# Expert rows weighted on their way out of PSUM and added onto the branch rows by accumulating scatters; the gate dot product as a 257th column

## What is computed

```
abel = gelu(xn @ abel_w + abel_b)
topw, topi = top_k(xn @ moe_gate_w + moe_gate_b, 2);  topw = softmax(topw)
eo[e] = gelu(xn @ ew1[e] + eb1[e]) @ ew2[e] + eb2[e]          # 8 experts, 256 -> 512 -> 256
moe  = sum of eo over a token's two experts, by their weights, times three matrix exponentials
gate = sigmoid(concat(abel, moe) @ gc_w + gc_b)
out  = layernorm-like result of (x + abel * (1 - gate) + moe * gate)
```

## Time and profile before

| | us |
|---|---|
| median of 3 runs (lowest, highest) | 943.55 (942.94, 944.96) |
| the profiled execution | 945.53 |
| its span, first to last instruction | 943.8 |
| PE busy in the span | 720.9 (76%) |
| DVE busy | 585.4 (62%) |
| ACT busy | 386.0 (41%) |
| POOL busy | 252.0 (27%) |
| mean granted clock of TensorE | 0.876 of full speed |

### The profile page before, as it was taken

How to read it: one execution, slowest core, us unless ns; L and a number is a source line. 1 busy time by engine, 2 the same in 40 slices (tenths; PEclk the granted TensorE clock), 3 DMA queues, 4 the chain that set the end, 5 groups by cost and what they waited for, 6 DMA issues and landing times. The chain is left out here.

```text
span 943.8 us, 15614 instructions
## 1 busy us (share of the span) xinstructions
PE 720.9 (76%) x4757; PEld 521.2 (55%) x4758; DVE 585.4 (62%) x1547; ACT 386.0 (41%) x637; POOL 252.0 (27%) x289
## 2 busy tenths in 40 slices
PE   4896759887988889897957308969999999947430
PEld 3785335545464636363635107858888888834220
DVE  5824476859686868879755154644545454507996
ACT  3221537563737365656532102334444444411223
POOL 1000120202516070615152130003333333322332
PEclk9999779999999989999979557989999999975555
DMA  5600223432717263453531128734434443219752
GB/s 156 215 0 0 45 80 54 113 66 85 163 36 188 47 173 76 143 105 108 119 91 68 46 98 276 259 57 104 102 84 102 90 109 80 70 32 346 234 190 89
DMA packets 144447, 106.13 MB, mean 112 GB/s; under 512 B 76416, under 2 KB 134667, under 8 KB 144396
## 3 DMA queue, kind: packets, MB, share of 16 engines
q1 hardware_dynamic: 127980, 75.85, 28.7%
q0 software_dynamic: 16416, 29.64, 13.4%
HBM read 55.05 MB, written 33.62 MB: 94 GB/s over the span
## 5 line engine op out<-in xcount | busy, mean ns | idle before, releaser
L1456 POOL DMA_INDIRECT scratch_ys<-ye,place x78 | 76.9, 986 | 197.8 <-ACT ye L1485 185.1
L52 PE MATMUL up<-xe_s,w_s 128*128 128x256 bf16 x936 | 110.9, 276 | 7.0 <-DMA xe_s<-scratch_zs 7.0
L52 PE MATMUL down<-w_s,h_s_e 128*128 x936 | 108.8, 273 | 0.3 <-DVE h_s_e L1521 0.3
L52 PEld LDWEIGHTS up<-xe_s,w_s 128*128 x936 | 92.7, 99 | 19.4 <-issue 7.5
L52 PEld LDWEIGHTS down<-w_s,h_s_e 128*128 128x128 bf16 x936 | 90.8, 98 | 12.4 <-issue 1.0
L52 PE MATMUL bank<-xn_s,mlp_w 128*128 128x512 bf16 x384 | 89.4, 392 | 10.3 <-DVE xn_s L702 10.3
L1518 DVE CAST h_s_e<-hf_e 128x512 bf16<-128x512 f32 x78 | 35.0, 448 | 98.7 <-ACT hf_e L1475 98.6
L391 POOL DMA_INDIRECT scratch_zs<-rows,pos x64 | 77.3, 1207 | 61.4 <-DVE pos L860 42.6
L52 PE MATMUL bank<-mlp_w,shared 128*128 128x256 bf16 x768 | 86.4, 273 | 2.2 <-DVE shared L758 2.2
L1475 ACT ACTIVATE hf_e<-up,eb 128x256 f32<-128x256 f32 x156 | 65.5, 471 | 48.0 <-PE up L52 47.4
L52 PEld LDWEIGHTS bank<-mlp_w,shared 128*128 128x128 bf16 x768 | 74.9, 98 | 12.7 <-DVE shared L758 2.7
(11 more groups left out here) (239 smaller groups left out, 1278.5 us busy)
## 6 DMA issues: line engine op xcount, KB each, us to landing
w_f<-in_ew SPq DMA_DIRECT2D x16, 512.0 KB, 5.5
got<-scratch_ys SPq DMA_DIRECT2D x16, 512.0 KB, 6.1
x_in<-in_x SPq DMA_DIRECT2D x8, 512.0 KB
x_ob<-in_out_b_row SPq DMA_DIRECT2D x8, 512.0 KB, 3.8
x_res<-in_mlp_b_row SPq DMA_DIRECT2D x8, 512.0 KB, 4.9
x_ob<-in_x POOLq DMA_DIRECT2D x8, 512.0 KB, 8.8
x_res<-in_x POOLq DMA_DIRECT2D x8, 512.0 KB, 10.9
x_res<-x POOLq DMA_DIRECT2D x8, 512.0 KB, 5.2
```

The lines of the kernel that those rows point to most:

```text
L52: last = nc.tensor.matmul(dst, lhs(a, k), rhs(b, k), start=start and n == 0, stop=stop and n == total - 1)
L1456: nc.gpsimd.indirect_dma_start(out=ys_dram[:, :], out_offset=bass.IndirectOffsetOnAxis(ap=place[:, k, s:s + 1], axis=0), in_=ye[:, k % 2, ...
```

## The change

The weights of a token's two experts are now made batch by batch in the first stage (`weigh`) and ride with the row into `zs`, negated, as two more tags. In the expert stage DVE reads from the tags which of the two weights a row needs, and ACT multiplies by it while it copies the row out of PSUM. POOL's scatters add (`compute_op=ALU.add`) onto `ys`, which has one row for each token and starts as the stored `abel` row, so that it ends as `abel - moe`. Since two tiles can add to the same row, POOL waits for the scatters of the tile before. The folded `eb2` is added inside the expert's PSUM group by a matmul over two rows (`ones2`, `eb2_s`). Every row has a 257th column: the weight stage appends `turnmat` times `gc_w` as a column, so that PE computes the gate's dot product with the row; `abel`'s part is stored as its row's 257th number. The rows of `eb2` are moved to one partition and split at the end of the weight stage. `abx` is loaded into SBUF at the end of the expert stage. The last stage has no PE work, no `weighted` and no difference on POOL. `dots` and `store_branch` of the first stage now follow each other, since the stored row holds the dot product.

```diff
+HOME, FIRST, SECOND_W, MORE_W = 2 * D, 2 * D + 2, 2 * D + 4, 2 * D + 6
+DG = D + 1
 ROW = 2 * D + 16
...
                         .then_inc(z4T_in, 16)
             def store_branch(j):
-                sp.wait_ge(gelu_r, TT * j + TT)
-                sp.dma_start(ab_dram[j].rearrange("(t p) d -> p t d", p=P), abel[j % 2])\
...
                 pool.wait_ge(rows_tail, j + 1)
...
                 nc.scalar.activation(az[:, :], az[:, :], ACT.Ln, bias=1.0).then_inc(lz_r, 1)
+                if i >= LAG:
...
+                    nc.vector.scalar_tensor_tensor(scrap[:, n], abel[j % 2][:, n, 0:D], -1.0, gc1_row[:, :], ALU.mult,
+                                                   ALU.mult, accum_out=abel[j % 2][:, n, D:DG]).then_inc(part_r, 1)
...
+                dve.wait_ge(gap_exp, j + 1)
+                link(nc.vector.tensor_scalar(wv[:, :], td[:, at], 1.0, None, ALU.add))
+                link(nc.vector.reciprocal(wv[:, :], wv[:, :]))
+                wait(dve, sent[j % 2], 16 * 2 * TT * (j // 2))
+                nc.vector.scalar_tensor_tensor(tag(SECOND_W), td[:, at], -1.0, wv[:, :], ALU.mult, ALU.mult)\
+                    .then_inc(weight_r, 1)
+                dve.wait_ge(weight_r, 2 * j + 1)
+                nc.vector.scalar_tensor_tensor(tag(MORE_W), wv[:, :], -1.0, tag(SECOND_W), ALU.mult, ALU.subtract)\
...
                     places(j)
...
+            sp.wait_ge(const_r, 5)
+            sp.dma_start(eb2[:, 0:D], t["eb2"]).then_inc(vec_in, 16)
...
+            sp.wait_ge(eb_r, 1)
+            for e in range(NE):
+                sp.dma_start(eb2_row[:, e * DG:(e + 1) * DG], eb2[e:e + 1, :]).then_inc(eb_moved, 16)
+            sp.wait_ge(eb_lo, 2)
+            sp.dma_start(eb2_s[1:2, :], eb2_lo[:, :]).then_inc(eb_moved, 16)
+            sp.wait_ge(eb_moved, 16 * NE + 16)
...
+            dve.wait_ge(eb_moved, 16 * NE)
+            nc.vector.tensor_copy(eb2_s[0:1, :], eb2_row[:, :]).then_inc(eb_lo, 1)
+            dve.wait_ge(eb_lo, 1)
+            nc.vector.tensor_tensor(eb2_lo[:, :], eb2_row[:, :], eb2_s[0:1, :], ALU.subtract).then_inc(eb_lo, 1)
...
+                    wait(pe, w2_r, m - RING + 1)
...
+            pe.wait_ge(turn_r, 1)
+            pe.wait_ge(vec_in, NV)
+            for k in range(KC):
+                last = nc.tensor.matmul(bank[6][0:NE, 0:DG], eb2t[:, k], turnmat[:, k], start=k == 0, stop=k == KC - 1)
+            last.then_inc(eb_done, 1)
...
+                sp.dma_start(tags[:, k], zs_dram[bass.ds(row, SLOT), HOME // 2:HOME // 2 + 4]
...
+            for b in range(BATCHES):
+                sp.dma_start(abx[:, b], abx_dram[b].rearrange("(t p) d -> p t d", p=P)).then_inc(abx_in, 16)
+            sp.wait_ge(abx_in, 16 * BATCHES)
...
         @block.gpsimd
         def _(pool):
...
+            for q in range(QT):
+                k = q % 4
+                pool.wait_ge(ye_r, ST * q + ST)
+                pool.wait_ge(placed, q + 1)
+                if q > 0:
+                    pool.wait_ge(ys_out[(q - 1) % 4], 16 * ST * ((q - 1) // 4 + 1))
                 for s in range(ST):
...
-                        in_=ye[:, k % 2, s, :], in_offset=None, bounds_check=2 * NTILES * P - 1, oob_is_err=False)\
-                        .then_inc(ys_out[k], 16)
-            over_tiles(pool, send)
+                        in_=ye[:, k % 2, s, :], in_offset=None, bounds_check=NTILES * P - 1, oob_is_err=False,
+                        compute_op=ALU.add).then_inc(ys_out[k], 16)
...
+                act.wait_ge(weight_r, q + 1)
...
-                nc.scalar.activation(ye[:, par], down_bank[par][:, :, :], ACT.Copy).then_inc(ye_r, 1)
+                for n in range(ST):
+                    nc.scalar.activation(ye[:, par, n], down_bank[par][n][:, 0:DG], ACT.Copy,
+                                         scale=weight[:, k, n:n + 1]).then_inc(ye_r, 1)
...
+                nc.vector.tensor_scalar(is_first[:, k], tag(FIRST - HOME, I32), tef[:, bass.ds(q, 1)], None,
+                                        ALU.is_equal).then_inc(first_r, 1)
+                nc.vector.tensor_tensor(place[:, k], tag(0, I32),
                                         nowhere[:, bass.ds(q, 1)].rearrange("p a s -> p (a s)"), ALU.max)\
                     .then_inc(placed, 1)
+                dve.wait_ge(first_r, 2 * q + 1)
+                nc.vector.tensor_tensor(is_first[:, k], is_first[:, k], tag(MORE_W - HOME, F32), ALU.mult)\
+                    .then_inc(first_r, 1)
+                dve.wait_ge(first_r, 2 * q + 2)
+                nc.vector.tensor_tensor(weight[:, k], is_first[:, k], tag(SECOND_W - HOME, F32), ALU.add)\
+                    .then_inc(weight_r, 1)
...
                 for n in range(ST):
-                    last = split_product(nc, down_bank[par][:, n], lambda s, k: h_s[:, par, s, k, n * P:(n + 1) * P],
-                                         lambda s, k: w2_s[:, s, bass.ds(e * (FC * D) + k * D, D)], FC)
+                    out = down_bank[par][n][:, 0:DG]
+                    nc.tensor.matmul(out, ones2[:, :], eb2_s[:, bass.ds(e * DG, DG)], start=True, stop=False)
+                    last = split_product(nc, out, lambda s, k: h_s[:, par, s, k, n * P:(n + 1) * P],
+                                         lambda s, k: w2_s[:, s, bass.ds(e * (FC * DG) + k * DG, DG)], FC, start=False)
...
             def load(b):
-                wait(sp, mix_r, TT * (b - IN + 1))
-                for r in range(2):
-                    sp.dma_start(got[:, b % IN, r], ys_v[r, b]).then_inc(rows_in[b % IN], 16)
-                sp.dma_start(abel[:, b % IN], rows_of(ab_dram, b)).then_inc(rows_in[b % IN], 16)
-                sp.dma_start(abx[:, b % IN], rows_of(abx_dram, b)).then_inc(rows_in[b % IN], 16)
+                if b >= 2:
+                    sp.wait_ge(less_in[b - 2], 16)
+                sp.dma_start(less[:, b], ys_v[b]).then_inc(less_in[b], 16)
...
-                act.wait_ge(sum_r, b + 1)
-                nc.scalar.activation(gate[:, b % 2], s2[:, b % 2], ACT.Sigmoid, bias=gc_b[:, :]).then_inc(gate_r, 1)
+                act.wait_ge(less_in[b], 16)
+                nc.scalar.activation(gate[:, b], less[:, b, :, D], ACT.Sigmoid, bias=gc_b[:, :], scale=-1.0)\
+                    .then_inc(gate_r, 1)
+                act.wait_ge(gate_r, b + 1)
+                nc.scalar.activation(back[:, b], gate[:, b], ACT.Copy, scale=-1.0).then_inc(back_r, 1)
...
+                if b + 3 < BATCHES:
+                    gates(b + 3)
...
-                dve.wait_ge(bias_done, b + 1)
-                dve.wait_ge(rows_in[b % IN], 64 * (b // IN + 1))
+                dve.wait_ge(back_r, b + 1)
                 wait(dve, res_r, TT * (b - MIX + 1))
                 for n in range(TT):
-                    nc.vector.scalar_tensor_tensor(moe[:, b % MIX, n], got[:, b % IN, 0, n],
-                                                   wtop[:, 0, b * TT + n:b * TT + n + 1],
-                                                   bias_bank[par][n // 2][:, n % 2], ALU.mult, ALU.add)\
-                        .then_inc(first_r, 1)
-                for n in range(TT):
-                    dve.wait_ge(first_r, TT * b + n + 1)
-                    nc.vector.scalar_tensor_tensor(moe[:, b % MIX, n], got[:, b % IN, 1, n],
-                                                   wtop[:, 1, b * TT + n:b * TT + n + 1],
-                                                   moe[:, b % MIX, n], ALU.mult, ALU.add).then_inc(moe_r, 1)
-                wait(dve, gate_r, b - 1)
-                wait(dve, part_r, TT * b)
-                for n in range(TT):
-                    dve.wait_ge(moe_r, TT * b + n + 1)
-                    nc.vector.scalar_tensor_tensor(scrap[:, n], moe[:, b % MIX, n], 1.0, gc2_row[:, :],
-                                                   ALU.mult, ALU.mult, accum_out=s2[:, par, n:n + 1])\
-                        .then_inc(part_r, 1)
-                dve.wait_ge(part_r, TT * (b + 1))
-                nc.vector.tensor_tensor(s2[:, par], s2[:, par], gate_part[:, b * TT:(b + 1) * TT], ALU.add)\
-                    .then_inc(sum_r, 1)
-            def mixed(b):
-                par = b % 2
-                dve.wait_ge(gate_r, b + 1)
-                dve.wait_ge(diff_r, b + 1)
-                for n in range(TT):
-                    nc.vector.scalar_tensor_tensor(moe[:, b % MIX, n], diff[:, par, n], gate[:, par, n:n + 1],
-                                                   abx[:, b % IN, n], ALU.mult, ALU.add).then_inc(mix_r, 1)
+                    nc.vector.scalar_tensor_tensor(mix[:, b % MIX, n], less[:, b, n, 0:D], back[:, b, n:n + 1],
+                                                   abx[:, b, n], ALU.mult, ALU.add).then_inc(mix_r, 1)
                 for n in range(TT):
...
-            weighted(1)
+            mixed(0)
             for b in range(BATCHES):
-                mixed(b)
-                if b + 2 < BATCHES:
-                    weighted(b + 2)
+                if b + 1 < BATCHES:
+                    mixed(b + 1)
```

(21 more changed lines are left out.)

276 lines of the change are left out of this document (117 added, 159 removed).

## The result

| | before | with the change |
|---|---|---|
| median, us (lowest, highest) | 943.89 (942.94, 944.96), 4 runs | 984.66 (982.38, 990.91), 4 runs |
| span of the profiled execution | 943.8 | 980.6 |
| mean granted clock | 0.876 | 0.883 |

The account below looks back on a forecast made before the run. PE was taken to bound the expert stage, DVE the last. Terms 4.5 + 1.0 + 1.5 + 11.5 + 25.3 + 1.5 - 58.8 = -13.5 us gave 932.0 profiled, 930.1 as median; range 913 to 968.

Parts of the forecast that it names:

- Expert stage, PE's term: Expert stage, PE: two-row matmuls and longer rows add 0.65 us a tile, making 5.89; +25.3 us over 39 tiles.
- the chain of the scatters: Expert stage, POOL: wake 0.85, both scatters 2.28, data 0.47 and 0.75, receipt 0.95; 5.30 us a tile, costed at nothing.
- the 6.24: Expert stage: scatter time per tile, in us, over which the changed kernel would be slower than before.
- The loads of `abx`: End of expert stage: 4 MB, 12 us at 341 GB/s, running beside PE's last two tiles and the scatters.
- Rival A: Expert stage: scatters complete in 3.2 us, not 2.2, so their 6.35 us a tile bounds; +18, 948 us; chance 0.35.
- the chain's own bounds, 3.9 and 8.6: Expert stage, us a tile: 3.9 if wake and receipt are half; 8.6 if completion takes 5.5 us.
- The estimate beside it: Expert stage scatters with the skill page's 2.0 us fixed DMA part: 0.85 + 2.28 + 2.0 + 0.75 = 5.9 us a tile.
- Rival B: Expert stage: two-row matmuls cost PE no bubble, a tile is 5.48 us, 914 us in all; chance 0.17.
- C: Weight stage's end: tail longer, single-row load issues at their 7.2 us bound; +4, 934 us; 0.10 shared with small terms.
- Weight stage, start: PE waits for the gated `turnmat` column and folds into `eb2` first, partly hidden: +1.5 us of 2.5.
- First stage: Four `weigh` steps on DVE, 0.75 us a batch for six batches, +4.5 us; last scatter later, +1.0.
- Last stage: DVE-bound: first load and gates 4.7, eight batches 27.6, end 7.1; 39.4 us in place of 98.2, -58.8.

## Why the prediction was wrong

The predicted 930.1 us is what the kernel takes without the adding (929.4) or without the wait (929.9). Point by point:

- **Expert stage, PE's term**: right. 5.91 a tile for 5.89, and 0.32 for a matmul over two rows as read from one place of another stage. It was not the bound.
- **The step that failed**: the chain of the scatters, summed to 5.30 us a tile, "under 5.89, so I cost it at nothing". It measured 7.17 and bounds the stage. The term of that sum which was wrong most is "both scatters take until 703.33, 2.28". This is the price of two plain scatters, taken for adding ones. The accumulating DMA was priced anew for its data, by the earlier trace rows, but not for its issue on POOL; the earlier trace rows is of an instruction that the change replaces. Adding issues measured 1.62 each, so 3.54 for the two in place of 2.28: +1.26 a tile.
- **The second miss, in the same sum**: data and completion together, with POOL's wake, came to 3.63 in place of 3.02: +0.61. With nothing beside the scatters it is 3.12 and 3.17, so most of this miss is the loads that share the DMA engines, which the sum left out. The parts were off in both directions: the data of the adds cost the engines three times the plain ones and not twice, receipt and wake cost less.
- With both, the chain is 7.17, 1.26 over PE's 5.91, and 38 steps of it make 48 of the 51.5 us by which the stage missed. The issues alone would have turned the sign: 5.30 + 1.26 is 6.56, over the 6.24 that the prediction gave for that. Of the other 3.6 us, 1.1 are the slower issues of the last tile and 0.4 lie ahead of the first scatter. Most of the rest is the step between the last two tiles, which was 3.06 us before and is 5.41 now.
- **The loads of `abx`** were costed at nothing beside PE's last two tiles. They held up two tiles of the chain, by 4.4 us together (9.96 and 8.88 against 7.20). In the mean of 7.17 this is hidden by the last three steps, 4.5 shorter in all.
- **Rival A** is what happened, in its place and its effect: the chain is the bound, and its first threshold, 5.89, measured 5.91; no run tests the second, 6.24. Its cause fits in part. It named a longer completion, by the receipt or by a collision with the transposed load; completion is 0.61 of the 1.87 us a tile, mostly the collision, and the issues are 1.26. It was given 0.35. It was kept small because the chain's own bounds, 3.9 and 8.6, varied wake and receipt but never the issue. (The lower one is a slip: half of 0.85 and 0.95 less is 4.4.) The chain that came lies inside these bounds, but the range left the upper one out. The range stopped at a chain of 6.86, 968 us, and missed by 17. The estimate beside it, from the Trainium skill's page "DMA: Bandwidth & Descriptors", put the chain at the edge with the same wrong 2.28; with the measured issue it is 0.85 + 3.54 + 2.0 + 0.75 = 7.14, an estimate within 0.03 of the trace, though in part by luck, since the measured 2.0 has POOL's wake in it and the data are longer.
- **Rival B** fell (0.32 us, not 0.109). **C** partly holds: issues 4.8 for 3.4, other parts of the tail shorter, the sum 12.6 for 11.5.
- **Weight stage, start**: +1.5 was written. From the last `zs` scatter to the end of PE's folds are 62.7 us before and 61.3 after, and between 60.8 and 64.1 in the other nine executions with this order of folds, so a loss of 1.5 can be neither seen nor ruled out. Behind the folds PE waits 19.15 us for the first tile, 7.03 before: the tail costs 12.1 of the 12.6 us that its steps take.
- **First stage**: 0.69 a batch for 0.75. The total of +7.8 has 2 to 3 us in it that no step explains and that lie within what this stage moves from run to run.
- **Last stage**: right but for the wait for the first store; 2.5 us in all.

Open: why an adding indirect scatter keeps POOL 0.6 us longer than a plain one. No run took it apart; the length of the row is excluded. It is also open how much the transposed loads cost the chain in every tile; two quiet tiles say about 0.5 us, and no run moved the loads.

## What to carry to other kernels

When a change turns an instruction into another form, price every resource of the new form: its issue on the engine, its data, its completion. Here the row of the old form was 0.6 us too low for each issue. When a wait for completion is put in a loop, write down the whole ring (wake, all issues, data, completion) against the loop's period. In this kernel a slow form that nobody waits for was free, and so was a wait on a fast one, as long as PE took longer. Where rows collide only because two producers share a destination, a second table with one add behind it can be cheaper than the ordering: here 938.5 against 984.7 us.

## What the runs showed of the hardware that was not expected

- An indirect scatter of 128 rows from GpSimd that adds keeps the engine 1.56 us, with means of 1.56 to 1.66 in the runs; one that writes keeps it 0.98, with means of 0.98 to 1.10, at the same row length.
- A tile's two adding scatters whose rows are all out of bounds still take 5.4 us from start to start, with 2.0 us between the last issue's end and the next start.
- The same adding scatter takes the DMA engines three times as long as a plain one: 34.9% against 11.7% of the 16 engines in 665:865, with 9771 packets against 3259 for the same 8 MB.
- The granted clock falls in parts of the stage once PE waits in it: it is 0.66 in 825:830 and 0.74 in 885:890, and 1.00 in nearly all other stretches of 5 us up to 880. The stage's mean is 0.94, and its `down` matmuls measure 287 ns on average against 273 before.
